# In-place conversion and later turning of the second layer's weights, and first-batch query projections from rounded parts, in a two-layer transformer kernel

## The reference, cut to what matters

```python
xn = _layernorm(x, ln_scale, ln_bias)                 # x: (2, 1024, 128)
q = (xn @ Wq)                                         # 16 heads of 64
k, v = split(xn @ Wkv)                                # 4 groups of 64
q = _layernorm(q, qn_scale, qn_bias)                  # over each head
k = _layernorm(k, kn_scale, kn_bias)
attn = softmax(einsum(q, k) * 64 ** -0.5)
out = einsum(attn, v) @ Wout
...
# second layer: Wu, Wv, Wb, Wo in float32; gate, up and down weights are int32, used as w_int.astype(float32) / 127
```

## Time and profile before

| | |
|---|---|
| runs | 862.07, 858.6, 861.04 us (median 861.04) |
| profiled execution | 859.0 us, its span 857.1 us |
| TensorE busy | 814.7 us, 95% of the span |
| VectorE, GpSimd, ScalarE busy | 622.0, 575.3, 470.6 us |
| granted TensorE clock, mean | 0.997 of full speed |
| batch 0: first unit of scores, first product with the values | 51.29 and 86.78 us |
| batch 1: first unit of scores, first product with the values | 402.82 and 437.21 us |

### The profile page before, as it was taken

The page is one execution under the profiler, slowest core; times in us unless marked ns, Lnnn a source line. Parts: engine busy times, 40 slices in busy tenths (PEclk is TensorE's granted clock), DMA queues, the critical chain, the costliest instruction groups (busy, mean ns, idle before and its releaser), DMA issues.

```text
span 857.1 us, 13613 instructions
## 1 busy us (share of the span) xinstructions
PE 814.7 (95%) x4924; PEld 449.6 (52%) x4924; DVE 622.0 (73%) x1041; ACT 470.6 (55%) x844; POOL 575.3 (67%) x376
## 2 busy tenths in 40 slices
PE   3888999999999999989889999999999999999998
PEld 3444444444444454456544454445444445986765
DVE  5668677877778877446877778777777777677763
ACT  2665555555555655767655565555566566455421
POOL 2645688768888778856567888767888777356410
PEclk9999999999999999999999999999999999999999
DMA  6000000000000000000000000000000001200001
GB/s 175 0 2 1 1 1 2 1 1 1 2 2 0 2 2 1 1 1 1 1 1 1 2 1 1 1 1 2 1 1 1 1 1 51 54 2 0 2 0 50
DMA packets 49597, 7.98 MB, mean 9 GB/s; under 512 B 42487, under 2 KB 47995, under 8 KB 49531
## 3 DMA queue, kind: packets, MB, share of 16 engines
q1 hardware_dynamic: 48666, 6.99, 5.2%
q10 hardware_dynamic: 864, 0.13, 0.1%
HBM read 5.92 MB, written 1.05 MB: 8 GB/s over the span
## 4 chain that ended last, share of the span: by engine, by line
PE 82%; DVE 11%; ACT 3%; POOL 2%; issue 2%; DMA 1%; DVEq 0%; SPq 0%; POOLq 0%; ACTq 0%
PE psum L692 27%; PE psum L677 19%; PE psum L657 12%; PE psum L707 4%; DVE part L1201 4%; PE psum L720 3%; PE psum L1721 3%; PE psum L1769 2%; PE psum L547 2%; PE psum L1759 1%; PE psum L1780 1%; DVE q_rate L1186 1%; DVE ql L1193 1%; PE psum L639 1%; ACT space L887 1%
## 5 line engine op out<-in xcount | busy, mean ns | idle before, releaser
L521 POOL TENSOR_TENSOR space<-space 128x1024 f32<-128x1024 f32 x160 | 380.2, 2376 | 26.9 <-ACT space L929 8.5
L1201 DVE TENSOR_REDUCE part<-psum 128x2 f32<-128x1024 f32 x256 | 313.0, 1223 | 113.8 <-PE psum L657 111.0
L929 ACT ACTIVATE space<-psum 128x512 f32<-128x512 f32 x512 | 264.4, 603 | 147.2 <-PE psum L677 128.1
L692 PE MATMUL psum<-space,vb 128*64 128x512 f32 x1024 | 247.5, 605 | 0.0
L657 PE MATMUL psum<-kh,qh 64*128 64x512 f32 x512 | 127.8, 495 | 12.4 <-DVE part L1201 10.0
L526 POOL TENSOR_TENSOR space<-space 128x1024 f32<-128x1024 f32 x30 | 71.6, 2387 | 97.3 <-DVE space L1217 97.3
L657 PEld LDWEIGHTS psum<-kh,qh 64*128 64x128 f32 x512 | 47.7, 183 | 143.8 <-DVE part L1201 109.7
L692 PEld LDWEIGHTS psum<-space,vb 128*64 128x64 f32 x1024 | 62.3, 136 | 106.1 <-issue 71.6
L677 PE MATMUL psum<-qh,kh 64*128 64x512 f32 x512 | 102.7, 395 | 0.0
L677 PE MATMUL psum<-qh,kl 64*128 64x512 f32 x512 | 101.6, 390 | 0.0
L677 PE MATMUL psum<-ql,kh 64*128 64x512 f32 x512 | 101.6, 390 | 0.0
(11 more groups left out here) (234 smaller groups left out, 961.9 us busy)
## 6 DMA issues: line engine op xcount, KB each, us to landing
ql<-nmx SPq DMA_DIRECT2D x256, 0.5 KB, 2.0
wproj<-in_L_ffn_W SPq DMA_DIRECT2D x4, 256.0 KB, 3.1
out<-x SPq DMA_DIRECT2D x4, 256.0 KB, 2.0
x<-in_L_attn_x SPq DMA_DIRECT2D x2, 256.0 KB, 4.9
wproj<-in_L_attn_Wq SPq DMA_DIRECT2D x1, 512.0 KB, 7.0
x<-in_L_attn_x SPq DMA_DIRECT2D x1, 512.0 KB, 7.9
wout<-in_L_attn_Wout SPq DMA_DIRECT2D x1, 512.0 KB, 7.0
w1s<-in_L_ffn_W SPq DMA_DIRECT2D x2, 256.0 KB, 2.7
```

The costliest lines, as they stand in the source:

```text
L521: pool.tensor_tensor(to, pt[0] if u == 1 else to, pt[u], ALU.add)\
L692: last = pe.matmul(outp[rows(h), :], vb[:, place(m)[1], kt, :], pt[kt][:, h, :], start=(kt == 0), stop=(kt == TILES - 1))
L929: act.activation(pt[kt][:, h, :], key_scores[kt % 2][h], ACT.Exp).then_inc(exp_made, 1)
L1201: dve.tensor_reduce(to[:, half, :], scores.rearrange("p (h k) -> p h k", h=2), AX_X, ALU.max, negate=True)\
```

## The change

1. `raw` becomes `wt` itself: the DMAs write there, the conversion is done in place, and the transposed tiles are copied back over the same columns. `work` stays free of them.
2. The two `turn_w` and the two `keep_w` move from batch 0's preparation to that of batch 1. On GpSimd the conversion moves behind `twin(0, 3)`.
3. In batch 0, tiles 2 to 7 of `norms` and 1 to 7 of `folded` (13 calls) use `project_split`. For this ScalarE makes `row_high`, `q_high` and `u_high` of batch 0 by three copies, and VectorE the low parts by three subtractions. Batch 1 makes its own again as before.

```diff
-        raw = work[:, 0:W_TILES * P]
-        rawi = work[:, W_TILES * P:W_TILES * P + (W_TILES - W_GATE) * P].bitcast(I32)
+        raw = wt[:, :]
+        rawi = wt[:, W_GATE * P:].bitcast(I32)
@@ GpSimd
             normal(0, 0)
+            twin(0, 3)
             pool.wait_ge(r_in, 16 * N_RAW)
             pool.tensor_scalar(raw[:, W_GATE * P:], rawi[:, :], SCALE1, 0.0, ALU.mult, ALU.add).then_inc(w_float, 1)
-            twin(0, 3)
@@ TensorE, norms
+                if n == 2:
+                    pe.wait_ge(x0_low_made, 1)
+                    pe.wait_ge(q0_low_made, 1)
-                    last = project_split(j, to, c["q_high"], c["q_low"], k) if b else project(b, j, to, Q_AT + k * 512)
+                    last = project_split(j, to, c["q_high"], c["q_low"], k) if b or j >= 2 else project(b, j, to, Q_AT + k * 512)
@@ TensorE, folded
+                if n == 1:
+                    pe.wait_ge(x0_low_made, 1)
+                    pe.wait_ge(u0_low_made, 1)
-                    last = project_split(j, to, c["u_high"], c["u_low"], k) if b else project(b, j, to, U_AT + k * 512)
+                    last = project_split(j, to, c["u_high"], c["u_low"], k) if n else project(b, j, to, U_AT + k * 512)
@@ TensorE, unit_scores
-                    pe.wait_ge(w_kept, 2)
+                    if b:
+                        pe.wait_ge(w_kept, 2)
@@ TensorE, the order
             turn_queries(0, 0)
-            pe.wait_ge(w_float, 1)
-            pe.wait_ge(kh_made, STEPS)
-            pe.wait_ge(kl_made, STEPS)
-            turn_w(0, 8)
             norms(0, 3)
             turn_queries(0, 1)
             folded(0, 3)
-            pe.wait_ge(w_kept, 1)
-            turn_w(8, W_TILES)
             produce(0)
...
             norms(1, 2)
+            pe.wait_ge(w_float, 1)
+            pe.wait_ge(kh_made, 2 * STEPS)
+            pe.wait_ge(kl_made, 2 * STEPS)
+            turn_w(0, 8)
             turn_queries(1, 0)
             folded(1, 2)
             norms(1, 3)
+            pe.wait_ge(w_kept, 1)
+            turn_w(8, W_TILES)
             turn_queries(1, 1)
@@ ScalarE, the order
             keep_values(0, 1)
+            act.wait_ge(xnt_made, 2)
+            act.activation(c["row_high"][0][:, :], xnt[:, 0, :], ACT.Copy).then_inc(x0_high_made, 1)
             guess_keys(0, 1)
...
             guess_keys(0, 2)
+            act.wait_ge(wq_centred, 1)
+            act.activation(c["q_high"][:, :], wproj[:, Q_AT:Q_AT + INNER], ACT.Copy).then_inc(q0_high_made, 1)
             high_keys(0, 1)
+            act.wait_ge(w_folded, 1)
+            act.activation(c["u_high"][:, :], wproj[:, U_AT:U_AT + INNER], ACT.Copy).then_inc(u0_high_made, 1)
             keep_folded(0, 0)
...
             high_queries(0, 0)
-            act.wait_ge(w_turned, 1)
-            keep_w(0, 8)
             square_queries(0, 3)
@@ VectorE, the order
             low_keys(0, 1)
+            dve.wait_ge(x0_high_made, 1)
+            dve.tensor_tensor(c["row_low"][0][:, :], xnt[:, 0, :], c["row_high"][0][:, :].bitcast(F32), ALU.subtract).then_inc(x0_low_made, 1)
+            dve.wait_ge(u0_high_made, 1)
+            dve.tensor_tensor(c["u_low"][:, :], wproj[:, U_AT:U_AT + INNER], c["u_high"][:, :].bitcast(F32), ALU.subtract).then_inc(u0_low_made, 1)
+            dve.wait_ge(q0_high_made, 1)
+            dve.tensor_tensor(c["q_low"][:, :], wproj[:, Q_AT:Q_AT + INNER], c["q_high"][:, :].bitcast(F32), ALU.subtract).then_inc(q0_low_made, 1)
             sum_keys(0, 3)
```

More of the change, by code:

```diff
@@ L308, in first_layer @@
         u_low_made = sem("u_low_made")
+        x0_high_made = sem("x0_high_made")
+        x0_low_made = sem("x0_low_made")
+        q0_high_made = sem("q0_high_made")
+        q0_low_made = sem("q0_low_made")
+        u0_high_made = sem("u0_high_made")
+        u0_low_made = sem("u0_low_made")
         rows0_summed = sem("rows0_summed")
@@ L1036, in scalar_part @@
             guess_queries(0, 3)
-            act.wait_ge(w_turned, 2)
-            keep_w(8, W_TILES)
             produce(0)
@@ L1068, in scalar_part @@
             square_queries(1, 2)
+            act.wait_ge(w_turned, 1)
+            keep_w(0, 8)
             high_queries(1, 0)
@@ L1072, in scalar_part @@
             square_queries(1, 3)
+            act.wait_ge(w_turned, 2)
+            keep_w(8, W_TILES)
             high_queries(1, 1)
```

## The result

The changed kernel takes 856.77 us (median of 20 runs), the kernel before 861.05 us on the same chips (20 runs): a ratio of 0.9947, 95% interval 0.9931 to 0.9963, so 4.3 us faster. On two other chips the same pair gave 0.9969 (0.9945 to 0.9993) and 0.9964 (0.994 to 0.9988), so some 3 us there. The profiled executions stand 3.3 us apart: spans of 857.1 and 853.8 us.

The account below looks back on a forecast made before the run. TensorE was taken to bound the kernel nearly everywhere, attention passing shifts on whole. Batch 0's −4.32 us and batch 1's +1.05 sum to −3.3; from 857.7 (median) and 856.9 (mean) it took 857.3 us, range 853.8 to 860.9.

Parts of the forecast that it names:

- What bounds the kernel: Whole kernel: TensorE bounds nearly everywhere, busy 95% of the span; attention passes any shift from the preparations on whole.
- First unit of scores: Batch 0's preparation: without turnings and copies, with split products, scores start at 48.07 instead of 51.29 us, 3.22 us earlier.
- the split latency: Batch 0's preparation: a split product reaches ScalarE in 1.68 instead of 1.92 us, 0.24 us less per tile where awaited.
- `produce(0)`: Batch 0, first unit of scores to first product with the values: split products take 34.39 instead of 35.49 us, 1.10 less.
- Subtractions: VectorE, batch 0: three subtractions, 3.67 us, almost fit 3.53 us of idle time ahead of `sum_keys(0, 3)`; counted as 0.
- upper bound of 6.3 us: VectorE, batch 0: if GpSimd blocks all three subtractions, each loses 2.06 us and `sum_keys(0, 3)` comes 6.3 us late.
- ScalarE's copies and GpSimd's conversion: Batch 0: three copies fall into ScalarE's idle time, and GpSimd's moved conversion has 2.5 us of cover; cost 0.
- Batch 1: Batch 1's preparation: taking both turnings and their copies loses 1.05 us, with bounds of 0.1 and 2.2 us.
- More: Rival: batch 1's turnings cost almost nothing (sum −4.2) or second-layer clock helps (−5.0); 854 to 856 us, chance 0.20.
- Less: Rival: slower subtractions (sum −1.7) or half clock in the preparation (−1.6) eat batch 0's gain; 859.4 us, chance 0.18.
- slower: Rival: batch 0's subtractions block with GpSimd, `sum_keys(0, 3)` 6.3 us late, sum +3.0, 864 us; chance 0.06.
- Doesn't do what it says: Rival: split products might not be shorter in batch 0, leaving a sum of −1.9; chance within the 0.18 for less gain.

Follow-up runs that it names:

- x1_moved: Kernel before with in-place conversion and both turnings with copies moved to batch 1, products left unsplit; ratio to before 0.9989 (0.9967 to 1.0011).
- x2_split: Kernel before with in-place conversion and batch 0's split products, copies and subtractions, turnings left in batch 0; ratio to before 0.9992 (0.9968 to 1.0017).
- x5_double: Changed kernel with VectorE's three subtractions of batch 0 done twice; ratio to before 1.0004 (0.9983 to 1.0025).
- x6_none: Changed kernel without both turnings and their copies, so second-layer weights stay untransposed; ratio to before 0.9944 (0.9924 to 0.9965).
- x0_after: The changed kernel run again, nothing altered, beside the separate parts; ratio to before 0.9969 (0.9945 to 0.9993).
- y0_after: The changed kernel run a third time, nothing altered, beside the versions with added waits; 860.03 us, ratio to before 0.9964 (0.994 to 0.9988).
- y1_after_pad: Changed kernel with 150 already met waits added at TensorE's start; 858.25 us, ratio to before 0.9968 (0.9944 to 0.9992).
- z1_before_pad90: Kernel before with 90 already met waits added at TensorE's start; 862.47 us in one execution.
- x3_gap: Changed kernel with the first turning in batch 0's TensorE idle time, the second in the first's batch 1 place; 857.26 us, ratio to before 0.9962.
- y3_gap_pad: Changed kernel, first turning in batch 0's idle time, second in the first's batch 1 place, 150 met waits at TensorE's start; 857.27 us, ratio 0.9946.

## Why the prediction was right, and where its sizes were off

**What bounds the kernel**: right. D and G, 583 us of attention, carried a shift of 5 and of 4 us without change (0.01 and 0.10 us). Only the preparations and the second layer made time.

**First unit of scores, −3.22 us forecast, −3.38 measured** (B). It was forecast at 48.07 us and stood at 47.63; 0.28 us of that is A, which starts the chain earlier and which I put down to chance: nothing that A waits for was changed, and over the 14 profiles A lies between 17.4 and 19.2 us. The steps hold: the split latency leads the high queries to 46.34, they end 1.12 us later, and the scores follow 0.17 us behind them. `x1_moved` gives 2.74 us of this to the move and leaves 0.64 us for the split. My sum had 0.24 us for it. Cut at `turn_queries(0, 1)`, 0.31 us of the 0.64 lie ahead of it (27.60 us from the first `sum_keys` in `x1_moved`, 27.29 changed): that is my term. The other 0.33 us lie behind it: without the split `folded(0, 3)` starts at 46.03, takes 1.88 us, and holds the scores to 47.85 in `x1_moved`, although the high queries were done at 47.35. `x2_split` gives the split 0.54 us by another route.

**`produce(0)`, −1.10 forecast, −1.31 measured** (C). Batch 1's stretch was the right model and F is now 34.21, the same as C's 34.18.

**Subtractions, 0 forecast, 0 measured**, 1.22 us each, where they were expected. The doubled version shows that the zero was cover and no low price. The upper bound of 6.3 us did not show. Of two instructions that meet it was GpSimd's that waited: its rate step at 31.97 took 0.91 us beside the subtraction of `q_low` (31.58 to 32.80), where the same step took 0.22 us before. The Trainium skill (SBUF — State Buffer, section "Who interferes with whom") has the later one blocked, and this row agrees. So does `x5_double`, where three rate steps in a row came behind a subtraction each and took 1.0 to 1.2 us instead of 0.2:

```profile
31.43 1.00 POOL L468 TENSOR_TENSOR q_rate<-q_rate 128x16 f32<-128x16 f32 x1 [2.90 <-ACT q_rate L917]
32.51 1.18 POOL L469 TENSOR_TENSOR q_rate<-q_rate 128x16 f32<-128x16 f32 x1
33.77 1.06 POOL L470 TENSOR_SCALAR q_rate<-q_rate 128x16 f32<-128x16 f32 x1
```

In the changed kernel it cost nothing, for `normal(0, 0)` had slack.

**ScalarE's copies and GpSimd's conversion, 0**: right, nothing behind them is late in B.

**Batch 1, +1.05 forecast, +0.72 measured** (E +0.90, F −0.18). The first turning took 0.05 us instead of 0.14: from `norms(1, 0)` to `turn_queries(1, 0)` it is 9.95 us, and 9.90 before. The second took its price; `x6_none` without turnings has 16.08, so both together cost 0.91 us. That F would give 0.18 back, I had not in the sum, and why it does stays open.

**The missing term, +1.08** (H). The sum treated the second layer as a shift only, apart from its clock. The terms that I had make −4.26 us at batch 1's first product with the values; the sum said −3.3. So the forecast of −3.3 for the profiled execution came out to the tenth (857.1 to 853.8), and that it did so is luck: errors of 1.0 us in the preparations (A 0.28, B 0.16, C 0.21, E and F 0.33) stood against 1.1 us lost at a load. That the load was delayed by an instruction transfer is what the rows and the paddings show.

**The rivals.** "More" fell by its mechanism: the second turning was not hidden, and the second layer's clock was the same (I, −0.02 us). "Less" and "slower" fell with the subtractions; half clock in the preparation did come in part of the executions, as "less" had it, but before has those too. "Doesn't do what it says" fell with C.

**The time.** The median over all executions moved by 4.3 us, the profiled one by 3.3. Executions at a mean clock of 0.997 or more have medians of 855.70 us (10 of the changed kernel) and, on another chip, 858.86 us (16 of the kernel before): 3.2 us apart. On one and the same chip it is 2.6 us (856.26, four of `x0_after`, beside these 16) and 3.4 us (855.63, two of `y0_after`, and 859.01, 15 of before). So the change gives about 3 us at full clock, and the rest of the 4.3 us is how often a stretch at half clock falls into an execution, which the sum didn't have. The prediction also took 4.3 us as the least that a measurement could tell from no change; all three intervals exclude no change, at some 3 us on two of the chips. Whether the gain is over 0.5%, which had a chance of 0.37, stays open: 0.53% by the ratio, 0.37 to 0.69% by its interval. The forecast of 857.3 us lay between the sum from the median of three executions (857.7) and from the mean of four (856.9).

## The stretches at half clock

They are the scatter of this kernel: the executions of the changed kernel run from 855.17 us at a clock of 0.998 to 861.89 at 0.994, and 859.5 is typical at 0.989. In the profiles they lie around 27 to 34, 43, 55 and 81 to 89 us and, in `y1_after_pad`, at 434 us, where the engines hand each other small pieces, and behind 790 us. With the one of 27 to 34 us B is 2.6 to 2.7 us longer (35.68 against 33.06); with shorter ones it is 1.5 us in `z1_before_pad90` and 1.1 us in `x5_double`. I is 62.8 us in before and changed, and 64.3 to 67.7 in variants with more of them: the windows of `x6_none` read

```profile
790.00:800.00 10.00, 9.30 (x34) 0.83 0.01 2
800.00:810.00 10.00, 10.00 (x56) 0.66 0.00 0
810.00:820.00 10.00, 10.00 (x77) 0.83 0.01 2
```

where the changed kernel has

```profile
790.00:800.00 10.00, 8.10 (x37) 1.00 0.00 0
800.00:810.00 10.00, 10.00 (x86) 1.00 0.01 2
810.00:820.00 10.00, 9.75 (x58) 0.83 0.00 0
```

`x6_none` is 1.9 us ahead of the changed kernel at the end of H (789.2 and 791.0 us), and its I is 5.0 us longer. The before kernel has such stretches too (0.66 in 815 to 820 us). Whether a variant brings more of them by the placing of its work or whether the few profiles and runs make it look so, these runs don't settle. `x1_moved`, `x2_split`, `x3_gap`, `x5_double`, `x6_none`, `y1_after_pad` and `y3_gap_pad` had no execution at 0.997 or above in 12 each, which speaks for the first.

## What to carry to other kernels

Before adding work, look for the engine's idle time ahead of what waits last, and count it as a budget: here 3.53 us of VectorE carried three operations of 1.14 us for nothing and the next three at full price, and a turning of 0.9 us was free in a gap of 1.7 us and cost 0.9 us where TensorE was packed. Cut both traces at the same instructions and compare stretch by stretch: the total agreed with the forecast to a tenth while 1.0 us of small errors and a missed term of 1.1 us stood against each other. When a stretch that nobody touched gets longer, look at the DMA view for transfers of instructions beside its loads, and test it by shifting the engine's list of instructions. And read from the trace where the shift has put the transfer: 56 added waits moved it by 0.4 us, which tested nothing.

## What the runs showed of the hardware

- The second of two loads of 256 KB each landed 1.07 us later (5.59 instead of 4.52 us from the first one's issue to their use) when one instruction transfer of 16 KB lay 3.18 us behind its issue; so in all seven profiles with the transfer at 2.5 to 3.6 us, and in none of the seven without. 150 waits that were already met, added over 700 us earlier on TensorE, moved it away, and 90 brought it about in the kernel before.
- TensorE's mean granted clock differs between executions of one kernel (0.989 to 0.998 over 20 of the changed kernel, 0.988 to 0.998 over 35 of before), and with it the time: 859.5 against 855.7 us.
- A GpSimd operation on 16 columns took 0.91 to 1.18 us beside a VectorE subtraction of two SBUF inputs that had started earlier (changed kernel, `x5_double`), and 0.20 to 0.22 us alone.
- Three float32r products in place of a float32 one were the faster way from the first product to ScalarE's start, 1.68 against 1.92 us for 1024 columns, in batch 0 (39.63 to 41.30 us) as in batch 1.
